# A decoder layer on one core: the mixture-of-experts tiles begin one slot sooner in the written-out order, and one group's scatters go two to a slot

## The reference, cut to what matters

```
x = layernorm(x + self_attention(x))        # 16 heads of 8; the projections are circulant 128x128 matrices
x = layernorm(x + cross_attention(x, ctx))  # similarity to 120 context rows, two softmaxes, a 512x128 projection
x = layernorm(x + experts(x))               # 8 routed experts, the best 2 of each token; 1 shared expert for all
```

## Time and profile before

| | |
|---|---|
| median of 3 runs | 417.7 us (415.71 to 418.52) |
| the profiled execution | 414.05 us |
| its span, from the first to the last instruction | 412.2 us |
| TensorE busy, share of the span | 343.5 us, 83% |
| VectorE | 285.4 us, 69% |
| ScalarE | 173.8 us, 42% |
| GpSimd | 154.6 us, 38% |
| mean granted TensorE clock | 0.967 of full speed |

### The profile page before, as it was taken

How to read it: one execution, slowest core, us unless ns; L and a number is a source line. 1 busy time by engine, 2 the same in 40 slices (tenths; PEclk the granted TensorE clock), 3 DMA queues, 4 the chain that set the end, 5 groups by cost and what they waited for, 6 DMA issues and landing times.

```text
span 412.2 us, 8364 instructions
## 1 busy us (share of the span) xinstructions
PE 343.5 (83%) x2415; PEld 221.6 (54%) x2415; DVE 285.4 (69%) x834; ACT 173.8 (42%) x498; POOL 154.6 (38%) x262
## 2 busy tenths in 40 slices
PE   1737877887988997798968798999999999999780
PEld 1223555665656666576647464555565555655440
DVE  3344477777778899869886767888776777777231
ACT  2122344444543553344442254444554555555213
POOL 9800022224223227723375526026743323223233
PEclk9999999999998999969998699999999999999996
DMA  4864654676557633310003000202321111110073
GB/s 92 176 208 122 187 161 121 198 204 170 171 147 200 184 90 97 90 37 24 22 27 123 14 19 27 53 21 67 105 64 38 48 39 39 45 35 19 3 207 99
DMA packets 53195, 39.09 MB, mean 95 GB/s; under 512 B 7719, under 2 KB 46730, under 8 KB 53147
## 3 DMA queue, kind: packets, MB, share of 16 engines
q1 hardware_dynamic: 50881, 34.33, 30.4%
q0 software_dynamic: 2272, 4.24, 3.1%
HBM read 26.05 MB, written 12.69 MB: 94 GB/s over the span
## 4 chain that ended last, share of the span: by engine, by line
PE 52%; DVE 21%; issue 8%; DMA 6%; POOL 6%; SPq 4%; ACT 2%; ACTq 0%; POOLq 0%; DVEq 0%
PE pT L1475 9%; PE pS L1475 9%; PE pM L1486 5%; DVE negmax L908 4%; PE pM L1282 3%; PE pO L1466 3%; DVE inv_den L924 3%; POOL rstd L620 2%; PE pT L1476 2%; PE pS L1476 2%; PE pO L1319 2%; PE pT L1306 2%; DVE stats L935 2%; PE pS L1296 1%; DMA X<-in_x 1%
## 5 line engine op out<-in xcount | busy, mean ns | idle before, releaser
L691 POOL DMA_INDIRECT ys<-sim_rhs,sim_add x39 | 38.0, 974 | 71.9 <-ACT sim_rhs L842 70.4
L742 ACT ACTIVATE PT<-pT 128x512 f32<-128x512 f32 x64 | 38.0, 593 | 33.6 <-PE pT L1306 32.8
L1475 PE MATMUL pT<-W,XH 128*128 (+1 forms) x94 | 50.9, 623 | 0.0
L908 DVE TENSOR_REDUCE negmax<-pS 128x4 f32<-128x512 f32 x64 | 43.4, 680 | 8.9 <-PE pS L1296 8.5
L1475 PE MATMUL pS<-W,XH 128*128 (+1 forms) x94 | 49.0, 603 | 0.0
L1296 PE MATMUL pS<-Kdiag,Qst 128*128 128x512 f32 x64 | 40.0, 632 | 5.7 <-DMA Kdiag<-parts_scr 4.4
L1045 DVE TENSOR_TENSOR PT<-pT,PT 128x512 f32<-128x512 f32 x47 | 32.4, 689 | 15.1 <-PE pT L1476 14.8
L618 POOL TENSOR_SCALAR vareps<-meanvar 128x1 f32<-128x1 f32 x32 | 8.6, 268 | 86.8 <-DVE meanvar L937 86.6
L828 ACT COPY XH<-pO 128x384 f32<-128x384 f32 x47 | 22.5, 478 | 43.7 <-PE pO L1468 40.9
L1486 PEld LDWEIGHTS pM<-W,XH 128*128 128x128 f32 x188 | 28.1, 191 | 18.9 <-issue 14.0
L640 POOL DMA_INDIRECT xs<-X,slot x32 | 32.9, 1029 | 8.2 <-issue 5.6
(11 more groups left out here) (260 smaller groups left out, 783.5 us busy)
## 6 DMA issues: line engine op xcount, KB each, us to landing
parts_scr<-qk_hi SPq DMA_DIRECT2D x16, 256.0 KB, 3.0
W<-in_L_ffn_w SPq DMA_DIRECT2D x16, 256.0 KB, 3.8
Qst<-parts_scr SPq DMA_DIRECT2D x32, 96.0 KB
Kdiag<-parts_scr SPq DMA_DIRECT2D x64, 48.0 KB
Kst<-parts_scr SPq DMA_DIRECT2D x32, 96.0 KB
Qdiag<-parts_scr SPq DMA_DIRECT2D x64, 48.0 KB
sim_add<-xs SPq DMA_DIRECT2D x39, 65.0 KB, 1.8
parts_scr<-qk_lo SPq DMA_DIRECT2D x8, 256.0 KB, 3.4
```

The source lines that it names most:

```text
L691: pool.indirect_dma_start(ys.ap(), bass.IndirectOffsetOnAxis(ap=XR[:, i % XRING, D:D + 1].bitcast(I32), axis=0), YO[:, i % RING, :], None, ...
L742: act.activation(PT[:, u % 3, :], pT[:, 0, :], ACT.Exp, scale=SCALE).then_inc(p_sb, 1)
L908: dve.tensor_reduce(out=negmax[:, b % 2, HG * j:HG * (j + 1)], in_=pS[:, u % 2, :].rearrange("p (g k) -> p g k", g=HG), axis=AX.X, op=ALU.max,
L1475: pe.matmul(bank, XH[:, 1 - p, 2 * P:3 * P], W[:, bass.ds(e_up * I2, I2)], start=True, stop=False)
```

## The change

`FFN_SLOT` goes from 67 to 66. Round m of the tiles is in slot 66 + m on all engines: round -1, which only turns over the input rows of tile 0, stands in slot 65 behind step 1 of batch 15, round 0 in slot 66 behind step 2, and so on; the common loop now holds the rounds to 6, and the loop behind it begins with round 7. VectorE's part of tile i moves with it, to slot 67 + i. The constants counted in rounds go up by one, which leaves the routing of group 3 where it was between the slots: `PAD_LOAD`, `LAST_ROUTING`, `LAST_COUNT`, `LAST_TILES`. `LAST_SCATTER` begins one result later and is even again from the result 6 on. The scatters of group 2 are spread 2, 2, 2, 2 over slots 67 to 70; they were 1, 1, 1, 1, 2, 2 over slots 67 to 72. `SHARED_*`, `UP_SLOTS`, `ROUTE_SLOT` and `EARLY_TILES` are the same in both.

```diff
-PAD_LOAD = 11
-LAST_ROUTING = {6: (0,), 7: (1,), 8: (2,), 9: (3,), 10: (4, 5), 11: (6,), 12: (7,), 13: (8,)}
-LAST_COUNT, LAST_TILES = 11, 14
-LAST_SCATTER = {3: (0, 1), 4: (2,), 5: (3,), 6: (4, 5), 7: (6,), 8: (7,)}
+PAD_LOAD = 12
+LAST_ROUTING = {7: (0,), 8: (1,), 9: (2,), 10: (3,), 11: (4, 5), 12: (6,), 13: (7,), 14: (8,)}
+LAST_COUNT, LAST_TILES = 12, 15
+LAST_SCATTER = {4: (0, 1), 5: (2, 3), 6: (4, 5), 7: (6,), 8: (7,)}
...
-FFN_SLOT = 67
+FFN_SLOT = 66
...
         def scatters(g, n):
 
             i = n - scatter_slot(g)
-            if g == NG - 2 and i >= G4:
-                return [k for k in (2 * i - G4, 2 * i - G4 + 1) if k < 2 * G4]
+            if g == NG - 2:
+                return [2 * i, 2 * i + 1] if 0 <= i < G4 else []
             return [i] if 0 <= i < 2 * G4 else []
```

## The result

The changed kernel took 420.96 us in the median of 20 runs, the kernel before 417.12 in 20 runs beside it. The ratio is 1.011, with a 95% interval from 1.008 to 1.014: slower, by 3.3 to 5.8 us, so by less than 2%. All ratios here leave out the slow executions, those over 1.5% above the fastest of their kernel, which leaves 3 of 12 for `f2_adds_behind`; its profile and that of `g3_after_tables_filled` are of executions left out.

What follows compares the result with a forecast made beforehand. The prediction took round 7's start, set by the last batches' chains woven with the first tiles, as the bound; +2.4 (late step 4) - 1.3 (waits gone) + 1.4 (clock) = +2.5, put on the median as 420.1 us, range 415.0 to 422.6.

Steps and rivals of the forecast that it cites:

- a new wait ahead of step 4: TensorE, batch 15: done with round 1 at 237.0, it waits some 3.6 us for the softmax A.
- Step 3 late by 3.4 us: TensorE, batch 15: round 0 moved ahead, mostly at half clock, makes this step end at 234.8, before 231.4.
- if steps 7 and 3 run at full clock: Sign on TensorE, slot 67: if seen, the whole prediction is wrong; no size given.
- A late by 4.7 us: Softmax of batch 15 on VectorE, behind tables and tile 0: step 4 begins at 240.65, before 235.95.
- What comes back, 1.3 us: TensorE up to round 7: waits for hidden rows (0.4), first load (0.3) and ScalarE's copy (0.6) go; bounds 0.7 to 1.4.
- X2 kept at 0.7: Batch 15's chain from step 7 to step 8: TensorE's wait of 0.7 us for X2 stays as before.
- GpSimd's cover: Slot 71: the 8 scatters end near 251, step 7's statistics near 252.5, so 1.5 us of cover and cost 0.
- The clock, 1.4 us: TensorE, rounds 2 and 3: the new wait brings a third stretch at half speed, +1.4 us; bounds 0 and +3.1.
- Rival 1: The earlier start fills TensorE's waits behind 228.26, at most 2.7 us, giving 415.0 us; chance 0.13.
- Rival 2: Step 4 of batch 15 is late but TensorE's clock holds: +1.1 us, 418.8 us; chance 0.22.
- Rival 3: Clock stays down as long as at 227.7, if waits break the work behind: +4.2, 421.9 us; chance 0.13.
- Rival 4: Nothing shows: X2 of batch 15 sets round 7's start in both orders, 417.7 us; chance 0.05.

Runs made afterwards that it cites:

- f2_adds_behind: The changed kernel with GpSimd's three late add_shared instructions moved behind its first results; ratio 1.0037 to the kernel before.
- g3_after_tables_filled: The changed kernel with matmuls of ones in TensorE's waits (slots 62, 65, 66, 68) and the early tables halved into slots 69 and 70; ratio 0.9912.
- e3: The changed kernel with 18 matmuls of ones, result unused, in TensorE's new wait ahead of step 4 of batch 15; ratio 1.0024 to the kernel before.
- f4: The changed kernel with VectorE's early tables (L1162 to L1173) moved from slot 67 to slot 70; ratio 0.9986 to the kernel before.
- g4: The changed kernel with TensorE's round 0 alone moved back behind steps 7 and 3 of slot 67; ratio 1.0044 to the kernel before.
- e4: The kernel before with the scatter change alone (two a slot in slots 67 to 70), tiles at their old place; ratio 0.9949.

## Why the prediction was right, and where its sizes were off

- **Direction and place.** The forecast was a net loss with a new wait ahead of step 4, ended by A. It came so, 4.68 us for 3.6.
- **Step 3 late by 3.4 us.** This term was too long. Step 3 began 2.2 us late (7.68 against 5.49), and VectorE's R behind step 7 was 2.0 late (7.94 from step 1, before 5.96). I had put the whole of round 0 into a stretch at half clock of 6.6 us. In the profile after, the stretch lasted 3.1 us (231.5 to 234.6); it was 3.4 in e3, f4 and g4. Why it ended sooner, no run shows. The second product ran mostly at full clock, and steps 7 and 3 wholly. The prediction had named just that, "if steps 7 and 3 run at full clock", as a sign that the whole is wrong. The sign came and the forecast stood, because the next term made up for it.
- **A late by 4.7 us.** It was 4.3, and that it is so near is luck. The sum was 3.5 (with 0.1 of wait) for the late step, 2.3 for tile 0, less 1.1, since A was to take 0.65 us for 1.77. Measured were 2.0, 3.6 and, less, 1.25. L648 did not meet A, as forecast, but tile 0's L1053, and cost 1.3 us there where the sum had 0.4 for the meeting. One error of 1.5 us and one of 1.3 stand against each other. What holds is the order that was forecast: VectorE idle until step 7, then the statistics, the tables, tile 0 and A in a row. The net loss at step 4 was 4.3 - 2.3, about 2.1, for 2.4.
- **What comes back, 1.3 us.** The step named as "X2 kept at 0.7" failed: the second L648 met X2's L978 (1.20 us beside one of 1.22 at 260.31), so 0.6 us was added, and 0.9 came back. The three other waits did go. GpSimd's cover ahead of the root of batch 15's second layer norm was 1.5 us, as summed.
- **The clock, 1.4 us.** The mis-sized term: e3 measures 1.95 us up to round 7, and 0.9% of the time. I had the stretch as 3.3 us at half clock; 4.5 us of work lay in it. The bound of 3.1 held.
- **The sum.** The profile shows +2.7 up to round 7 and 3.1 in all, for 2.5. The median moved by 3.8, from 417.1 to 421.0, and the interval is 3.3 to 5.8; the forecast of 420.1 lies 0.9 below the median measured. I had put 0.13 on over 1%; the ratio lies at that mark.
- **Two parts taken as one.** I costed the scatters at the load's 0.35 us. They are worth 2.4 us up to round 7 alone and 4.2 with the early tiles. That the first load is in time for the earlier round 7 is the new spread's doing alone.
- **The rivals.** Rival 1, the filled waits, fell with the wait of 4.68 us; in g4, where step 3 came 2.8 us sooner, 2.44 of it were left. Rival 2, that the clock holds, fell with the 6.7 us at 0.50; e3 shows its time, +0.8 us up to round 7 for the 1.1 summed. Rival 3 had the stretch right, 6.7 us of which 2.2 were idle, but neither its price (3.1 us, where e3 measures 1.95) nor its condition: the work behind the wait was not broken by waits (none from 244.11 to 260). Rival 4 is excluded by the interval.

## What to carry to other kernels

When work is moved one place forward in an order written by hand, follow it on every engine. Ahead of TensorE's longest wait it moved one small turning of rows, but behind that it put a whole round ahead of step 3, and on VectorE 2.3 us ahead of the link that everyone waited for. Before filling waits or keeping the clock up, ask what else covers the same stretch: matmuls of ones were worth 2 us in the new wait and 0.2 in the old ones. When a forecast comes out, compare its terms and its own signs of being wrong with the trace: here two terms were off by over 1 us and cancelled. And a short instruction of one engine that holds up another is not mended by moving it; look where it lands.

## What the runs showed of the hardware

A VectorE instruction that begins while GpSimd issues a scatter can be held over the instruction behind it as well. L1053 at 241.47 began within the scatter from 240.71 to 241.67 and ended at 243.18, 0.29 behind the end of L648 (241.69 to 242.89). L1189 in f2 began at 275.62 within a result's DMA issue and ended at 277.59, L648 at 277.54; it is a 128x32 instruction, of 0.19 to 0.35 us elsewhere. With nothing of GpSimd close behind the scatter, A was held only to the scatter's end (236.74 in e4, the scatter's 236.71). The Trainium skill ("SBUF — State Buffer", section "SBUF: two separate sides") gives the pair of ports, shared by VectorE and GpSimd, to whoever starts first, for the whole instruction. In these rows VectorE started 0.2 to 0.7 us ahead of L648 and still came behind it. That the scatter held the ports when VectorE's instruction began, and L648 took them over from it, would fit; no run tests it. L1045, which has one operand in PSUM, took 0.67 to 0.69 us in every row of these stretches.
